# Score rows for the cluster attention from one weight-times-weight matrix per head, on one Trainium2 core

## The chip, the cores and the metric

The kernel runs on one core of one Trainium2 chip. A core has five engines, each with a queue of its own that is worked off in order: TensorE (PE in the profile; its weight loads are PEld), VectorE (DVE), ScalarE (ACT), GpSimd (POOL) and SyncE (SP), which issues the transfers. Engines meet only through semaphores. The metric is the device time of one execution in microseconds; lower is better.

## The reference, cut to what matters

32 images of 96 channels and 56x56 pixels are normalised over the channels, go through an attention with 8 heads of 48 features, and then through a feed-forward layer with quantised groups. The attention folds each image into four quarters of 28x28 pixels and works on each alone. In each quarter and head, 16 centers are the mean features of 7x7 blocks, and every pixel is compared with them:

```
f = einsum('bchw,dc->bdhw', x, Wf) + bf          # 384 features = 8 heads x 48
centers = _adaptive_avg_pool(f, 4, 4)            # 16 per head and quarter
cen_n = cen / maximum(norm(cen), EPS)
tok_n = tok / maximum(norm(tok), EPS)
sim = sigmoid(sim_beta + sim_alpha * einsum('bmc,bnc->bmn', cen_n, tok_n))
idx = argmax(sim, axis=1); sim = sim * one_hot(idx)
```

The masked `sim` then gathers the values of the pixels per center and spreads them back; `x + attention` goes on as tokens into the feed-forward layer (W1, gelu, W2, each with an absolute maximum over a group of six images).

The score of a pixel x against a center with pooled input p is x' Wf_h' Wf_h p (bias as a 97th row). The kernel never forms it from features: it makes a score row `Q` of 97 numbers for each of 8x16 centers, scales it by alpha over the center's norm, and multiplies it with the pixels.

## The kernel before, in words

A step works on one quarter. There are 128 quarters: five groups of 24 (six images, as the feed-forward layer's groups want it), and 8 more. Within a group `pipeline` runs slots; in each slot every engine runs a list of steps in the order that `attention` returns for it. A step has a phase (X first, then M, A, R) and a lag, so that one slot works on up to five quarters at once: X prepares a quarter (normalise, pool, centers, score rows), M computes features and scores, A masks, aggregates and spreads, R is the feed-forward layer's first half (tokens, their normalisation, the hidden tiles and their maxima). After the 24 slots of a group, `second_pass` runs the feed-forward layer's second half. In the groups after the first, a slot also finishes a quarter of the group before (`finish` on DVE, `clipped` on POOL). The order in an engine's queue is written out by hand; `done(engine, name, q)` makes that engine's queue wait until quarter q has passed the named step, and everything queued behind waits with it.

The steps that the change touches, in the order of the data, with the lines of the profile:

- `pooled` (DVE, L672): sums of the 16 blocks, `cenx`, 97x16.
- `centers` (PE, L925): features of the centers, 4 products with `wfT`.
- `centers` (DVE, L681): copies them to `cbd`, masked by head.
- `center_squares` (POOL, L394): `csq`, their squares.
- `center_products` (PE, L933 and L936): column sums of `csq` (the norms), and `cbd` times `wf` (the score rows), both into PSUM bank 0.
- `center_floor` (DVE, L688) and `center_norms` (POOL, L436): maximum with a floor, power -1/2.
- `q_scaled` (DVE, L693), `q_back` (PE, L958, a transposition), `q_placed` (DVE, L699): `Q`, used by `scores` of the next slot.

Around them on DVE stand `cosine` (L717, scores from PSUM times pixel norms, into `cosb`), then `residual` (L755, twice, which adds the attention's output to the image, with a hidden maximum L774 between), then `maxima` (L722, `top`). On PE, `features(0, 1)` (L969) is the next quarter's first feature tile. It writes the PSUM bank that `cosine` reads, so it begins with

```
if t0 == 0:
    done(pe, "cos_done", q - 1)
```

where q - 1 is the quarter that `cosine` handles in the same slot. `to_tokens("t")` (L906) needs `t_done` of both quarters of an image's half: in every other slot it needs the residual of this very slot.

Of the kernel before, what the change touches and what calls it, by code (L numbers as in the profile page):

```python
# [12 lines left out]
HM = HEADS * CENTERS  # L13
# [22 lines left out]
POOL_SETS = 7  # L36
DVE_SUMS, DVE_SIGNS, DVE_ALL = 4, 20, 24
# [23 lines left out]
def build(nc, x, Wf, bf, Wv, bv, Wp, bp, alpha, beta, W1, b1, W2, b2, consts, out):  # L61
# [3 lines left out]
    with ctx:  # L65
# [15 lines left out]
        cenx = sb("cenx", [C + 1, 4, CENTERS])  # L81
        cbd = sb("cbd", [C, 2, 4, 2, CENTERS])
        csq = sb("csq", [C, 2, HM])
        cn2 = sb("cn2", [HM, 2])
        cinv = sb("cinv", [HM, 2])
# [32 lines left out]
        wf = sb("wf", [C, 4, C + 1])  # L118
# [34 lines left out]
        def early(rows, *shape):  # L153
# [12 lines left out]
        NAMES = """x_side x_T x_stats x_sum x_dif x_half x_d2 x_v x_var x_rstd x_shift x_norm0 x_norm xn_ps0 xn_ps xn_copied0 xn_copied cen_x cen_f cen_bd  # L166
            cen_sq q_ps cen_n2 cen_inv q_scaled q_T q_done s_ps n2_done n2_floor n_newton0 n_square0 n_part0 n_factor0 n_newton1
# [91 lines left out]
        def _(sp):  # L259
            per_row = [(cst[:, :], consts), (w1[:, :, :], W1[0:G1 * GROUPS, :].rearrange("(g r) c -> r g c", g=GROUPS)),  # L260
                       (w2[:, :, :], W2[0:G2 * GROUPS, :].rearrange("(g r) f -> r g f", g=GROUPS)),
                       (wf[:, :, 0:C], Wf.rearrange("(k r) c -> r k c", k=4)),
                       (wv[:, :, 0:C], Wv.rearrange("(k r) c -> r k c", k=4)),
                       (wf[:, :, C:C + 1], bf.rearrange("(k r a) -> r k a", k=4, a=1)),
# [85 lines left out]
        def _(pool):  # L350
# [6 lines left out]
            nc.gpsimd.memset(uT[:, :, :, :], 0.0).then_inc(pool_set, 1)  # L357
            pool.wait_ge(pool_set, POOL_SETS)

# [28 lines left out]

            def center_squares(k, q, place, use):
                b = k % 2  # L390
                done(pool, "cen_bd", q)
                done(pool, "q_ps", q - 2)
                v = cbd[:, b, :, :, :].rearrange("c k h m -> c (k h m)")
                nc.gpsimd.tensor_tensor(csq[:, b, :], v, v, ALU.mult).then_inc(S["cen_sq"], 1)  # L394
# [36 lines left out]

            def center_norms(k, q, place, use):
                b = k % 2
                done(pool, "cen_n2", q)
                done(pool, "q_done", q - 2)
                nc.gpsimd.tensor_tensor(cinv[:, b:b + 1], cn2[:, b:b + 1], halfpow[0:HM, 0:1], ALU.pow).then_inc(S["cen_inv"], 1)  # L436
# [19 lines left out]
            def attention(g, part):  # L456
                return [(X, 1, moments("x", EPS_C)), (M, 1, norm_guess), (M, 1, newton), (M, 1, cubic),
                         (X, 1, center_squares), (R, 0, clipped(g, part), FINAL), (X, 1, center_norms),
                        (A, 0, marks), (R, 0, moments("t", EPS_T), FFN)]
# [18 lines left out]
        def _(act):  # L478
# [80 lines left out]
            def attention(part):  # L559
                return [(R, 1, normalise("t", 6, 1), FFN), (A, 1, copy_sim(0)), (R, 1, n_high(0, part), FFN),  # L560
                        (A, 1, copy_sim(1)), (R, 1, n_high(1, part), FFN), (X, 1, normalise("x", 0, 0)),
                        (X, 1, normalise("x", 0, 1)), (X, 1, copy_x(0)), (X, 1, copy_x(1)),
# [40 lines left out]
        def _(dve):  # L603
# [38 lines left out]
            for i in range(2):  # L642
                step(v.tensor_copy(V[:, 2 * i:2 * i + 2, :, 0:C],
                                   bank(4 + i, C + 1, 4 * C).rearrange("c (k h o) -> c k h o", k=2, h=2)))
            step(v.tensor_copy(w1T[0:C, 0:G1 * GROUPS], bank(6, C, G1 * GROUPS)))
# [21 lines left out]
            def pooled(k, q, place, use):  # L667

                done(dve, "xn_copied", q)
                done(dve, "u_done", q - 4)  # L670
                blocks = xn[:, k % 2, :].rearrange("c (a r b w) -> c a b r w", a=4, r=PW, b=4)
                v.tensor_reduce(cenx[:, k % 4, :].rearrange("c (a b) -> c a b", a=4), blocks, AX.XY, ALU.add)\  # L672
                    .then_inc(S["cen_x"], 1)

            def centers(k, q, place, use):

                done(dve, "cen_f", q)
                done(dve, "q_ps", q - 2)
                f = bank(0, C, 4 * CENTERS).rearrange("r (k m) -> r k m", k=4)
                mask = const("head_of_row", C)  # L680
                v.tensor_tensor(cbd[:, k % 2, :, :, :], f.unsqueeze(2).broadcast_to([C, 4, 2, CENTERS]),  # L681
                                mask.unsqueeze(1).unsqueeze(3).broadcast_to([C, 4, 2, CENTERS]), ALU.mult)\
                    .then_inc(S["cen_bd"], 1)

            def center_floor(k, q, place, use):
                done(dve, "q_ps", q)
                done(dve, "cen_inv", q - 2)
                v.tensor_scalar(cn2[:, k % 2:k % 2 + 1], bank(0, HM, 1, 64), NORM_FLOOR * AREA * AREA, None, ALU.max)\  # L688
                    .then_inc(S["cen_n2"], 1)

            def q_scaled(k, q, place, use):
                done(dve, "cen_inv", q)
                v.tensor_scalar(qT[:, :], bank(0, HM, C + 1, 128), cinv[:, k % 2:k % 2 + 1], alphac[:, :],  # L693
                                ALU.mult, ALU.mult).then_inc(S["q_scaled"], 1)

            def q_placed(k, q, place, use):
                done(dve, "q_T", q)
                done(dve, "s_ps", q - 2)
                v.tensor_copy(Q[:, k % 2, :], bank(0, C + 1, HM, 256)).then_inc(S["q_done"], 1)  # L699
# [31 lines left out]
            def summed(k, q, place, use):  # L731
                done(dve, "u_ps", q)
                done(dve, "a_ps", q - 1)
                sums = cenx[:, k % 4, :].unsqueeze(1).broadcast_to([C + 1, HEADS, CENTERS])
# [84 lines left out]
            def attention(g, part):  # L819
# [3 lines left out]
                         (X, 1, pooled), (R, 1, h_largest(4, 5), FFN), (M, 1, cosine), (X, 1, centers), (A, 1, residual(0)),  # L823
                         (R, 1, h_largest(5, 6), FFN), (A, 1, residual(1)), (X, 1, center_floor),
# [38 lines left out]
        def _(pe):  # L863
# [5 lines left out]
            mm(bank(1, G2, GROUPS), ones[0:G2, 0:G2], wsum2[:, :], start=True, stop=True)  # L869
            for k in range(4):  # L870
                tr(bank(2, C + 1, C, k * C), wf[:, k, :], ident[0:C, 0:C])
# [3 lines left out]
            for k in range(4):  # L875
                mm(bank(4 + k // 2, C + 1, 2 * C, k % 2 * 2 * C), wv[:, k, :],
                   wph[:, k, :, :].rearrange("r h o -> r (h o)"), start=True, stop=True)
            for g in range(GROUPS):
# [42 lines left out]
            def centers(k, q, place, use):  # L921
                done(pe, "cen_x", q)
                done(pe, "xn_copied", q)
                for c in range(4):
                    ins = mm(bank(0, C, CENTERS, c * CENTERS), wfT[:, c * C:(c + 1) * C], cenx[:, k % 4, :],  # L925
                             start=True, stop=True)
                ins.then_inc(S["cen_f"], 1)

            def center_products(k, q, place, use):

                done(pe, "cen_bd", q)
                done(pe, "cen_sq", q)
                mm(bank(0, HM, 1, 64), csq[:, k % 2, :], ones[0:C, 0:1], start=True, stop=True)  # L933
                n = 2 * CENTERS
                for c in range(4):
                    ins = mm(ps[c * n:(c + 1) * n, 0, 128:128 + C + 1],  # L936
                             cbd[:, k % 2, c, :, :].rearrange("r h m -> r (h m)"), wf[:, c, :], start=True, stop=True)
                ins.then_inc(S["q_ps"], 1)
# [17 lines left out]
            def q_back(k, q, place, use):  # L956
                done(pe, "q_scaled", q)
                tr(bank(0, C + 1, HM, 256), qT[:, :], ident).then_inc(S["q_T"], 1)  # L958
# [102 lines left out]
            def attention(g):  # L1061
# [5 lines left out]
                        (X, 1, centers), (A, 1, spread(1)), (M, 0, features(0, 1)), (X, 1, center_products), (X, 1, end_of_group(g), FFN),  # L1067
# [70 lines left out]
```

## Time and profile before

| | |
|---|---|
| median of 3 runs | 3020.39 us (3018.07 to 3020.47) |
| span of the profiled execution, first to last instruction | 3014.8 us |
| PE busy (matmuls / weight loads) | 95% / 64% of the span |
| DVE busy | 89% |
| ACT busy | 72% |
| POOL busy | 67% |
| mean granted TensorE clock | 0.988 of full speed |

The profiled execution has no other time than its span on the page; the median of the runs is 5.6 us longer. A row of a timeline is one or several like instructions: start, duration, engine, line, operation, tiles and shapes, and in brackets how long the engine had been idle before and what ended that. Consecutive instructions of one engine overlap a little in the records, so that the time that an instruction takes in its queue is better read from its start to the next one's start.

### The profile page before, as it was taken

Reading aid. Unit: us, or ns where it says so; the run is one execution under the profiler, and the core shown is the slowest. Engines: PE = TensorE matmul, PEld = TensorE weight load, DVE = VectorE, ACT = ScalarE, POOL = GpSimd, SP = SyncE. Lnnn points to the kernel's source line nnn. Section 1 sums busy time; section 2 is a strip of 40 time slices with the busy share of each in tenths; the row PEclk is TensorE's granted clock in tenths of the full one; section 3 lists DMA queues with packets and bytes.
Section 4 is the critical chain, followed back from the end, with each engine's and each line's share of the span. In section 5 each row is a group of like instructions: output and inputs, shape, how many; then the busy total and the mean of one; then the engine's idle time right before and its main releaser. Section 6 shows DMA issues by size and latency. Waiting matters only on the chain.

```text
span 3014.8 us, 62753 instructions
## 1 busy us (share of the span) xinstructions
PE 2860.9 (95%) x20998; PEld 1934.8 (64%) x20998; DVE 2683.4 (89%) x5540; ACT 2177.4 (72%) x4510; POOL 2014.7 (67%) x4275
## 2 busy tenths in 40 slices
PE   3999999999999999999999999999999999999987
PEld 2666666556666665666666566666665666666554
DVE  3788888999999989999999999999999999998975
ACT  1677777897767779777777886777789777777952
POOL 1566666677777768777777347777767777776354
PEclk9999999999999999999999999999999999999997
DMA  1011111002222210122222012222200222221034
GB/s 45 17 40 34 33 33 33 9 17 65 66 65 65 65 49 1 49 65 65 66 73 65 10 33 70 74 68 65 57 25 17 65 65 65 66 65 49 1 94 132
DMA packets 30932, 154.29 MB, mean 51 GB/s; under 512 B 6483, under 2 KB 6804, under 8 KB 30612
## 3 DMA queue, kind: packets, MB, share of 16 engines
q1 hardware_dynamic: 30612, 150.28, 17.8%
q8 instruction: 169, 2.77, 0.4%
q14 instruction: 151, 1.24, 0.1%
HBM read 75.60 MB, written 74.66 MB: 50 GB/s over the span
## 4 chain that ended last, share of the span: by engine, by line
POOL 58%; issue 21%; PE 13%; DVE 4%; ACT 3%; POOLq 1%; SPq 0%; DMA 0%; DVEq 0%; ACTq 0%
POOL eq L442 7%; POOL mo_x L384 6%; POOL mo_t L384 6%; PE ps L1102 4%; PE ps L1046 4%; POOL turns L468 4%; POOL tok L452 3%; POOL mo_x L379 3%; ACT turns L579 2%; POOL cinv L436 2%; POOL n2c L399 2%; DVE turns L844 2%; POOL csq L394 2%; PE ps L969 1%; POOL nxy L411 1%
## 5 line engine op out<-in xcount | busy, mean ns | idle before, releaser
L969 PE MATMUL ps<-wfT,xn 97*112 97x384 f32 x1792 | 735.9, 518 | 0.3 <-ACT sq L523 0.2
L1046 PE MATMUL ps<-tok,w1T 98*128 98x392 f16 x2880 | 599.7, 330 | 13.5 <-ACT turns L582 8.7
L523 ACT ACTIVATE sq<-ps 112x384 f32<-112x384 f32 x896 | 431.0, 489 | 207.8 <-PE ps L969 204.8
L468 POOL CAST turns<-turns 128x392 f16<-128x392 f32 x240 | 324.9, 1367 | 206.1 <-ACT turns L579 201.9
L1046 PEld LDWEIGHTS ps<-tok,w1T 98*128 98x128 f16 x2880 | 269.5, 97 | 226.1 <-issue 61.1
L707 DVE TENSOR_REDUCE n<-sq 112x32 f32<-112x1536 f32 (+1 forms) x256 | 396.0, 1547 | 20.9 <-ACT sq L523 6.8
L774 DVE TENSOR_REDUCE hmax<-ps 128x1 f32<-128x392 f32 x720 | 382.1, 558 | 33.7 <-PE ps L1046 28.1
L969 PEld LDWEIGHTS ps<-wfT,xn 97*112 97x112 f32 x1792 | 271.7, 180 | 213.9 <-DVE cosb L717 65.5
L529 ACT ACTIVATE sig<-cosb,betac 112x896 f32<-112x896 f32 x128 | 133.3, 1041 | 312.2 <-DVE cosb L717 312.2
L492 ACT ACTIVATE xnT<-ps,mo_x 112x96 f32<-112x96 f32 x896 | 304.4, 454 | 62.2 <-POOL mo_x L386 62.2
L579 ACT ACTIVATE turns<-ps,scale 128x1176 f32<-128x1176 f32 x240 | 323.0, 1346 | 36.1 <-DVE scale L797 34.5
L844 DVE SCALAR_TENSOR_TENSOR turns<-turns 128x1176 f16<-128x1176 f32 x240 | 330.2, 1376 | 0.0
L1102 PE MATMUL ps<-turns,w2T 128*96 128x392 f16 x1440 | 287.6, 336 | 22.9 <-DVE turns L844 22.8
L492 ACT ACTIVATE nT<-ps,mo_t 112x96 f32<-112x96 f32 x840 | 283.5, 438 | 28.5 <-POOL mo_t L386 28.4
L442 POOL TENSOR_TENSOR eq<-sig,top 112x896 bf16<-112x896 f32 x128 | 219.2, 1713 | 49.8 <-DVE top L722 49.8
L977 PE MATMUL ps<-Q,xn 97*112 97x128 f32 x1792 | 228.2, 279 | 24.0 <-ACT sq L523 24.0
L1102 PEld LDWEIGHTS ps<-turns,w2T 128*96 128x96 f16 x1440 | 160.0, 123 | 134.3 <-DVE turns L844 90.4
L394 POOL TENSOR_TENSOR csq<-cbd 96x128 f32<-96x128 f32 x128 | 50.7, 396 | 268.4 <-DVE cbd L681 268.4
L1009 PE MATMUL ps<-sim,xnT 112*97 112x128 f32 x1792 | 227.4, 279 | 2.4 <-ACT turns L545 2.3
L977 PEld LDWEIGHTS ps<-Q,xn 97*112 97x112 f32 x1792 | 202.5, 177 | 42.4 <-ACT sq L523 42.4
L1029 PE MATMUL ps<-turns,aggp 128*96 128x448 f32 (+1 forms) x512 | 217.6, 507 | 1.3 <-DVE aggp L746 1.3
L1009 PEld LDWEIGHTS ps<-sim,xnT 112*97 112x97 f32 x1792 | 200.1, 164 | 16.6 <-ACT turns L545 4.7
(143 smaller groups left out, 6125.8 us busy)
## 6 DMA issues: line engine op xcount, KB each, us to landing
xbuf<-in_x SPq DMA_DIRECT2D x64, 588.0 KB, 4.6
out<-xbuf SPq DMA_DIRECT2D x64, 588.0 KB, 6.0
turns<-out SPq DMA_DIRECT2D x60, 588.0 KB, 6.3
out<-turns SPq DMA_DIRECT2D x60, 588.0 KB, 4.4
tok<-in_L_ffn_W SPq DMA_DIRECT2D x2, 142.5 KB
cst<-in_constants SPq DMA_DIRECT2D x1, 195.0 KB
wf<-in_L_conv_Wf SPq DMA_DIRECT2D x1, 144.0 KB
tok<-in_L_conv_Wv SPq DMA_DIRECT2D x1, 144.0 KB
```

The lines of the kernel that those rows point to most:

```text
L442: nc.gpsimd.tensor_tensor(heads(eq[:, :]), heads(sig[:, k % 2, :]), over_centers(top[:, :]), ALU.subtract)\
L468: nc.gpsimd.tensor_copy(ghi[:, k % 3, HT:2 * HT], gel[:, k % 3, HT:2 * HT]).then_inc(b_mid, 1)
L492: ins = nc.scalar.activation(dst, bank(b0 + part, TN, C, (t - t0) * C), ACT.Identity, bias=m[:, 9, t:t + 1], scale=m[:, 8, t:t + 1])
L523: nc.scalar.activation(sq[:, t, :], bank(2 + t % 2, TN, D), ACT.Square).then_inc(f_sq, 1)
L579: nc.scalar.activation(gel[:, k % 3, :].rearrange("p (c n) -> p c n", c=FC), ps[:, h:h + 3, 0:HT], ACT.Gelu, scale=scale[:, 0:1]).then_inc ...
L707: ins = v.reduce_sum(n2[:, t0 * HEADS:t1 * HEADS], sq[:, t0:t1, :].rearrange("p t (h d) -> p (t h) d", d=HD), AX.X)
L844: v.scalar_tensor_tensor(glo[:, k % 2, :], gel[:, k % 3, :], QCLIP, ghi[:, k % 3, :], ALU.min, ALU.subtract).then_inc(b_lo, 1)
L969: mm(bank(2 + t % 2, TN, D), xn[:, k % 2, t * TN:(t + 1) * TN], wfT[:, :], start=True, stop=True)\
L977: ins = mm(tile_bank(2, TN, HM, t), xn[:, k % 2, t * TN:(t + 1) * TN], Q[:, k % 2, :], start=True, stop=True)
L1009: ins = mm(bank(4, C + 1, HM), xnT[:, k % 4, t, :], sim[:, k % 2, t * HM:(t + 1) * HM], start=t == 0, stop=t == T - 1)
L1046: ins = mm(dst, w1T[:, c * 128:(c + 1) * 128], tok[:, bass.ds(place, 1), part, s * HT:(s + 1) * HT].rearrange("p a n -> p (a n)"), start=p ...
L1102: ins = mm(bank(6 + k % 2, C, HT), w2T[:, c, :], part[:, s, c * HT:(c + 1) * HT], start=n == 0, stop=n == 2 * FC - 1)
```

## The change

For each head, a matrix G = Wf_h' Wf_h (97x97, bias included) is made once at the start: 8 products on PE and two copies on DVE, with `wf` laid out by heads. `center_products` then makes the unscaled score rows straight from `cenx` and G (8 products of 97x32 weights, as `project` does it elsewhere), with a padded `cenx` in place of the masked `cbd`, at the place in PE's queue where `centers` stood. The steps `centers` (PE and DVE), `center_squares` and `center_floor` go. New are: `spread_centers` (POOL, `cenx` repeated for 8 heads into `cenr`), `copy_products` (ACT, score rows to SBUF, `qU`), `centers_turned` (PE, a transposition of `cenr`, at the place where `center_products` stood, behind `features(0, 1)`), and on DVE `center_norms`, which multiplies the turned centers with the score rows and sums over the 97 columns: that sum is the squared norm. It stands where `centers` stood on DVE, between `cosine` and `residual(0)`. POOL now does the floor itself, ahead of the power.

```diff
+            def center_norms(k, q, place, use):
+
+                done(dve, "cen_T", q)
+                done(dve, "q_side", q)
+                done(dve, "cen_floor", q - 2)
+                b = k % 2
+                v.tensor_tensor_reduce(cprod[:, :], bank(0, HM, C + 1, 256), qU[:, :], 1.0, 0.0, ALU.mult, ALU.add,
+                                       accum_out=cn2[:, b:b + 1]).then_inc(S["cen_n2"], 1)
...
-                         (X, 1, pooled), (R, 1, h_largest(4, 5), FFN), (M, 1, cosine), (X, 1, centers), (A, 1, residual(0)),
-                         (R, 1, h_largest(5, 6), FFN), (A, 1, residual(1)), (X, 1, center_floor),
+                         (X, 1, pooled), (R, 1, h_largest(4, 5), FFN), (M, 1, cosine), (X, 1, center_norms), (A, 1, residual(0)),
+                         (R, 1, h_largest(5, 6), FFN), (A, 1, residual(1)),
...
+            def spread_centers(k, q, place, use):
+                done(pool, "cen_x", q)
+                done(pool, "cen_T", q - 1)
+                nc.gpsimd.tensor_copy(heads(cenr[:, :]), cenx[:, k % 4, 1, :].unsqueeze(1).broadcast_to([C + 1, HEADS, CENTERS]))\
+                    .then_inc(S["cen_r"], 1)
...
+            def copy_products(k, q, place, use):
+                done(act, "q_ps", q)
+                done(act, "q_scaled", q - 1)
+                nc.scalar.copy(qU[:, :], bank(0, HM, C + 1, 128)).then_inc(S["q_side"], 1)
...
+            for h in range(HEADS):
+                mm(bank(h // 4, C + 1, C + 1, h % 4 * (C + 1)), wf[:, h, :], wf[:, h, :], start=True, stop=True)
...
-            def centers(k, q, place, use):
+            def centers_turned(k, q, place, use):
+                done(pe, "cen_r", q)
+                done(pe, "q_side", q)
+                tr(bank(0, HM, C + 1, 256), cenr[:, :], ident[0:C + 1, 0:C + 1]).then_inc(S["cen_T"], 1)
+
+            def center_products(k, q, place, use):
                 done(pe, "cen_x", q)
                 done(pe, "xn_copied", q)
...
+                n, turned = 2 * CENTERS, cenx[:, k % 4, :, :].rearrange("c s m -> c (s m)")
+                for h in range(2):
+                    for c in range(4):
+                        ins = mm(ps[c * n:(c + 1) * n, 0, 128:128 + C + 1], turned[:, (1 - h) * CENTERS:(1 - h) * CENTERS + n],
+                                 G[:, 2 * c + h, :], start=h == 0, stop=h == 1)
                 ins.then_inc(S["q_ps"], 1)
...
-                        (X, 1, centers), (A, 1, spread(1)), (M, 0, features(0, 1)), (X, 1, center_products), (X, 1, end_of_group(g), FFN),
+                        (X, 1, center_products), (A, 1, spread(1)), (M, 0, features(0, 1)), (X, 1, centers_turned), (X, 1, end_of_group(g), FFN),
```

On PE, in a slot of a middle group, from the last hidden tile (L1046, after: L1053) to the image's tokens (`xbuf`), the queue was

```order
L1046 MATMUL ps<-tok,w1T 128x392 x2
L925 MATMUL ps<-cenx,wfT 96x16 x4
L1029 MATMUL ps<-turns,aggp 96x336
L969 MATMUL ps<-wfT,xn 112x384
L933 MATMUL ps<-cst,csq 128x1
L936 MATMUL ps<-wf,cbd 32x97 x4
L969 MATMUL ps<-wfT,xn 112x384
L906 MATMUL ps<-cst,xbuf 112x96 x7
```

and it is, at the same place,

```order
L1053 MATMUL ps<-tok,w1T 128x392 x2
L943 MATMUL ps<-G,cenx 32x97 x8
L1036 MATMUL ps<-turns,aggp 96x336
L976 MATMUL ps<-wfT,xn 112x384
L935 MATMUL ps<-cst,cenr 128x97
L976 MATMUL ps<-wfT,xn 112x384
L917 MATMUL ps<-cst,xbuf 112x96 x7
```

The score rows moved ahead of the first feature tile (`wfT,xn`); what stands behind it now is the transposition of `cenr`.

On DVE, in the same slot, from `cosine` (`cosb`) to the scaled score rows (`qT`), the queue was

```order
L717 TENSOR_TENSOR cosb<-ps,ninv 112x896
L681 TENSOR_TENSOR cbd<-ps,cst 96x128
L755 SCALAR_TENSOR_TENSOR xbuf<-ps,bpc,xbuf 96x16x28
L774 TENSOR_REDUCE hmax<-ps 128x1
L755 SCALAR_TENSOR_TENSOR xbuf<-ps,bpc,xbuf 96x12x28
L688 TENSOR_SCALAR cn<-ps 128x1
L722 TENSOR_REDUCE top<-sig 112x56
L693 TENSOR_SCALAR qT<-ps,cinv,alphac 128x97
```

and it is

```order
L725 TENSOR_TENSOR cosb<-ps,ninv 112x896
L695 ISA cprod,cn<-ps,qU 128x97
L695 ISA cn 128x1
L763 SCALAR_TENSOR_TENSOR xbuf<-ps,bpc,xbuf 96x16x28
L782 TENSOR_REDUCE hmax<-ps 128x1
L763 SCALAR_TENSOR_TENSOR xbuf<-ps,bpc,xbuf 96x12x28
L730 TENSOR_REDUCE top<-sig 112x56
L701 TENSOR_SCALAR qT<-qU,cinv,alphac 128x97
```

Two single instructions went (`cbd`, `cn`), and two came: the product with its sum, and a second instruction that writes the sum out. They stand in front of both residuals, and they wait for the PE row `cst,cenr`.

## Rows read from the trace of the kernel before

**Rows 1.** The profile's page, parts 1 and 2: busy us and share; granted clock by slices.
```profile
span 3014.8 us, 62753 instructions
PE 2860.9 (95%) x20998; PEld 1934.8 (64%) x20998; DVE 2683.4 (89%) x5540; ACT 2177.4 (72%) x4510; POOL 2014.7 (67%) x4275
...
PEclk9999999999999999999999999999999999999997
```

**Rows 2.** Timeline of DVE, one slot of a middle group: start, us, instruction [idle before].
```profile
1919.23 1.08 DVE L717 TENSOR_TENSOR cosb<-ps,ninv 112x896 f32<-112x896 f32 x1
1920.22 0.28 DVE L681 TENSOR_TENSOR cbd<-ps,cst 96x128 f32<-96x128 f32 x1
1920.42 0.67 DVE L755 SCALAR_TENSOR_TENSOR xbuf<-ps,bpc,xbuf 96x448 f32<-96x448 f32 x1
...
1921.96 0.14 DVE L688 TENSOR_SCALAR cn<-ps 128x1 f32<-128x1 f32 x1
1922.03 1.07 DVE L722 TENSOR_REDUCE top<-sig 112x56 f32<-112x896 f32 x1
...
1927.00 1.25 DVE L663 BATCH_NORM_STATS2 st_x<-ps 112x6 f32<-112x96 f32 x7 [0.19 <-PE ps L906]
...
1931.62 1.19 DVE L766 TENSOR_TENSOR tok<-ps,tok 98x448 f16<-98x448 f32 x2 [0.17 <-ACT tok L556]
1933.02 0.29 DVE L735 SCALAR_TENSOR_TENSOR uT<-cenx,ps 97x128 f32<-97x128 f32 x1 [0.21 <-PE ps L1009]
...
1935.05 1.04 DVE L774 TENSOR_REDUCE hmax<-ps 128x1 f32<-128x392 f32 x2 [0.23 <-PE ps L1046]
...
1937.50 1.08 DVE L717 TENSOR_TENSOR cosb<-ps,ninv 112x896 f32<-112x896 f32 x1
```

**Rows 3.** Timeline of PE, the same slot.
```profile
1915.31 0.54 PE L1019 MATMUL ps<-V,uT 97*32 97x97 f32 x16
...
1918.89 0.85 PE L925 MATMUL ps<-cenx,wfT 97*96 97x16 f32 x8
1919.59 0.79 PE L1029 MATMUL ps<-turns,aggp 128*96 128x336 f32 x2
1920.37 0.90 PE L969 MATMUL ps<-wfT,xn 97*112 97x384 f32 x2
...
1921.71 0.90 PE L969 MATMUL ps<-wfT,xn 97*112 97x384 f32 x2
1922.45 0.74 PE L906 MATMUL ps<-cst,xbuf 96*112 96x96 f32 x7
1923.03 1.47 PE L969 MATMUL ps<-wfT,xn 97*112 97x384 f32 x4
1924.33 0.27 PE L958 MATMUL ps<-cst,qT 128*97 128x128 f32 x1
...
1931.21 1.77 PE L1009 MATMUL ps<-sim,xnT 112*97 112x128 f32 x14
```

**Rows 4.** Timeline of POOL, the same slot.
```profile
1923.18 1.71 POOL L442 TENSOR_TENSOR eq<-sig,top 112x896 bf16<-112x896 f32 x1 [0.42 <-DVE top L722]
...
1928.13 0.21 POOL L386 TENSOR_TENSOR mo_t<-mo_t 112x7 f32<-112x7 f32 x1
```

**Rows 5.** Timeline of ACT, the same slot.
```profile
1920.34 1.04 ACT L529 ACTIVATE sig<-cosb,betac 112x896 f32<-112x896 f32 x1 [2.51 <-DVE cosb L717]
...
1928.37 2.36 ACT L492 ACTIVATE nT<-ps,mo_t 112x96 f32<-112x96 f32 x7 [0.22 <-POOL mo_t L386]
```

**Rows 6.** The chain that ended last, whole span: the same place of the first group's slots.
```profile
146.30 2.58 issue
...
548.26 2.58 issue
```

**Rows 7.** The same chain, from 20 to 60 us: the preparation of the weights.
```profile
33.43 2.88 PE ps L876 x8
...
40.47 0.57 DVE V L643
```

More of the change, by code:

```diff
@@ L35 @@
 LOADS = 14
-POOL_SETS = 7
-DVE_SUMS, DVE_SIGNS, DVE_ALL = 4, 20, 24
+POOL_SETS = 8
+DVE_SUMS, DVE_SIGNS, DVE_ALL = 4, 20, 26
 CONSTS = {}
@@ L80, in build @@
         xn = sb("xn", [C + 1, 2, QN])
-        cenx = sb("cenx", [C + 1, 4, CENTERS])
-        cbd = sb("cbd", [C, 2, 4, 2, CENTERS])
-        csq = sb("csq", [C, 2, HM])
+        cenx = sb("cenx", [C + 1, 4, 3, CENTERS])
+        cenr = sb("cenr", [C + 1, HM])
+        qU = sb("qU", [HM, C + 1])
+        cprod = sb("cprod", [HM, C + 1])
         cn2 = sb("cn2", [HM, 2])
+        cfl = sb("cfl", [HM, 2])
         cinv = sb("cinv", [HM, 2])
@@ L387, in moments @@
                 return step
[L389 to L394, printed above, removed]
             def norm_guess(k, q, place, use):
@@ L457, in attention @@
                 return [(X, 1, moments("x", EPS_C)), (M, 1, norm_guess), (M, 1, newton), (M, 1, cubic),
-                         (X, 1, center_squares), (R, 0, clipped(g, part), FINAL), (X, 1, center_norms),
+                         (X, 1, spread_centers), (R, 0, clipped(g, part), FINAL), (X, 1, center_norms),
                         (A, 0, marks), (R, 0, moments("t", EPS_T), FFN)]
@@ L644, in _ @@
                                    bank(4 + i, C + 1, 4 * C).rearrange("c (k h o) -> c k h o", k=2, h=2)))
+            for i in range(2):
+                step(v.tensor_copy(G[:, 4 * i:4 * i + 4, :],
+                                   bank(i, C + 1, 4 * (C + 1)).rearrange("c (h o) -> c h o", h=4)))
             step(v.tensor_copy(w1T[0:C, 0:G1 * GROUPS], bank(6, C, G1 * GROUPS)))
@@ L671, in pooled @@
                 blocks = xn[:, k % 2, :].rearrange("c (a r b w) -> c a b r w", a=4, r=PW, b=4)
-                v.tensor_reduce(cenx[:, k % 4, :].rearrange("c (a b) -> c a b", a=4), blocks, AX.XY, ALU.add)\
+                v.tensor_reduce(cenx[:, k % 4, 1, :].rearrange("c (a b) -> c a b", a=4), blocks, AX.XY, ALU.add)\
                     .then_inc(S["cen_x"], 1)
-            def centers(k, q, place, use):
[L677 to L689, printed above, removed]
+            def center_norms(k, q, place, use):
[5 more added lines that the diff above has]
+                                       accum_out=cn2[:, b:b + 1]).then_inc(S["cen_n2"], 1)
             def q_scaled(k, q, place, use):
                 done(dve, "cen_inv", q)
-                v.tensor_scalar(qT[:, :], bank(0, HM, C + 1, 128), cinv[:, k % 2:k % 2 + 1], alphac[:, :],
+                done(dve, "q_T", q - 1)
+                v.tensor_scalar(qT[:, :], qU[:, :], cinv[:, k % 2:k % 2 + 1], alphac[:, :],
                                 ALU.mult, ALU.mult).then_inc(S["q_scaled"], 1)
@@ L877, in _ @@
                    wph[:, k, :, :].rearrange("r h o -> r (h o)"), start=True, stop=True)
+            for h in range(HEADS):
+                mm(bank(h // 4, C + 1, C + 1, h % 4 * (C + 1)), wf[:, h, :], wf[:, h, :], start=True, stop=True)
             for g in range(GROUPS):
```

40 lines of the change are left out of this document (16 added, 24 removed).

## The prediction, made before the changed kernel was run

> **What bounds the kernel now.** I began with the page's busy shares [rows 1]: TensorE is busy 95% of the span, VectorE 89%. So full an engine invites the thought that work taken off it is time won. But a busy TensorE is not one at its peak, so I went on to the timelines of one slot, engine by engine, and asked at each place who waits for whom.
>
> A slot takes 18.27 us: from one `cosine` to the next it is 1937.50 - 1919.23 [rows 2]. In the first group it is the same, (548.26 - 146.30) / 22 = 18.27 [rows 6], though VectorE and GpSimd have less to do there (nothing to finish, nothing to clip). So neither of these two is bound by the sum of its work. What both kinds of slot share is a ring of waits, which the rows show link by link. I set `cosine`'s start to 0 (1919.23):
>
> - `cosine` runs to 1.08; behind it on VectorE stand `cbd` at 0.99, the first residual at 1.19, the second, the floor `cn` at 2.73, and `top` at 2.80 to 3.87 [rows 2].
> - GpSimd's `eq` starts at 3.95, having idled 0.42 for `top` [rows 4]. The moments of the tokens follow without a pause and end at 9.11.
> - ScalarE starts `nT` at 9.14, having idled 0.22 for these moments [rows 5]. Behind `nT` in its queue stands the copy of the turned similarities, and for that copy TensorE's aggregation (L1009) waits; it starts at 11.98 [rows 3].
> - VectorE's `uT` waits 0.21 for the aggregation, and its hidden maxima 0.23 for the hidden tiles behind it on TensorE [rows 2]. From there VectorE runs through to the next `cosine` at 18.27.
>
> Every handover has an engine idle just before it, so the ring has no slack. It passes through VectorE's stretch from `cosine` to `top`, 2.80 us. Whatever makes this stretch longer makes the slot longer by as much, and TensorE's feature tiles, the turning of the marks and the scores are not on the ring at all: they only have to be done in time.
>
> **The change, part by part.**
>
> *TensorE.* The features of the centers took 0.70 (1918.89 to 1919.59) [rows 3]; the 16 passes that replace them have the shape of `project` (L1019), 0.54. The stretch from one feature tile to the next, with the norms and the score rows between, is 1.34 (1920.37 to 1921.71). A feature tile alone is 0.65, half of the 1.30 that two take (1923.03 to 1924.33), and a transposition as L958 lasts 0.27, so it becomes at most 0.92. TensorE sheds 0.58 a slot at least. But L1029 ends and `features(0, 1)` then waits for `cosine` in either kernel (it starts 0.06 behind it, at 1.14), so what is saved in front of it turns into a longer wait, and what is saved behind it lies off the ring. I count it as nothing.
>
> *VectorE, the work.* `cbd` goes: 0.20 from its start to the residual's. `cn` goes: 0.07 to `top` [rows 2]. The product with its sum is an instruction that this trace does not have. The order shows it as two, one of 128x97 and one of a single column. The nearest rows are the two that go: 0.20 and 0.07, 0.27 together, if both overlap with what follows as those do; 0.28 + 0.14 = 0.42 if they are worked off one after the other. I take 0.35, since the second reads what the first leaves. The Trainium skill says the same of the pair ("VectorE: DVE Perf Modes", the section on two Vector instructions with no wait between them: an operation that also writes its accumulator out is two instructions); it gives no time for the second, and no row here has one.
>
> *VectorE, the wait.* This is the term that decides. `center_norms` stands right behind `cosine` on VectorE. It waits for `centers_turned`, which stands on TensorE behind `features(0, 1)`, which waits for `cosine`. So VectorE sends its result to TensorE and can go on only when TensorE has done a whole feature tile and a transposition: 1.08 (end of `cosine`) + 0.06 + 0.65 + 0.27 = 2.06, and 0.04 more until VectorE starts (`uT` starts 0.04 behind the end of L1009 in the trace, 1933.02 against 1931.21 + 1.77) [rows 2, 3]. The product starts at 2.10, where `cbd` started at 0.99. Queued behind it are both residuals, a hidden maximum and `top`.
>
> The residual then starts at 2.10 + 0.35 = 2.45 in place of 1.19. From it to `cn` it is 1.54 (1920.42 to 1921.96), so `top` starts at 3.99 in place of 2.80. **The ring grows by 1.19**, from 18.27 to 19.46. With 0.27 and 0.42 for the product it is 1.11 and 1.26.
>
> *The covers.* The turned centers also need two other engines. ScalarE copies the score rows: these are done at 1918.89 + 0.54, that is 0.20, while ScalarE idles for `cosine` until 1.11 [rows 5]. Even at the price of the `sig` behind it (1.04 for nine times the columns) the copy ends at 1.28, before the 1.79 at which TensorE wants it. GpSimd repeats the centers as soon as the pooled sums are there, by -0.34 (L925 waited for the same); at the price of `eq` (1.71, a far larger tile) that is 1.4, still in time. Floor and power come after the product, 2.45; at 1.71 for both they end by 4.2, and `qT` is not wanted before `top` ends at about 5. In every other slot the tokens on TensorE wait for the second residual, which now ends near 3.99; they started at 3.22, so TensorE is 0.8 late there, less than the 1.19 that the ring gives it.
>
> *Outside the slots.* G costs 8 products of 97 columns at the start; the four of 192 there take 2.88 [rows 7], so about 2.9, and two copies of 0.57 and a few transpositions: +4.5, once. The 12 quarters' slots that have no feed-forward half (4 at the start, 8 at the end) are not on the ring. There TensorE's saving may count and the same stall may too: between -1.2 and +1.2 for each, ±14 in all; I take -2 for them, a little toward the saving, as there is little else on the engines there.
>
> *The sum.* 120 slots x 1.19 = 143, + 4.5 - 2 = 145 on the span of 3014.8: 3160. The median of the runs lies 5.6 above the span; I leave that as it is: 3020.4 + 145 = **3165**.
>
> **The rivals.**
>
> *A: TensorE is the bound.* It is 95% busy, and sheds 0.58 a slot: -0.58 x 120 = -70, +4.5, so 2955. For it speaks the share; against it the ring, and that `features(0, 1)` waits for `cosine` anyway. It decides if the aggregation on TensorE was waiting for its own queue and not for ScalarE, and if VectorE can take in 1.1 of idle time. VectorE's idle time in a slot is 0.19 + 0.17 + 0.21 + 0.23 = 0.80 [rows 2], less than that, so I give it 4%.
>
> *B: only VectorE's own time counts.* If the link through GpSimd and ScalarE had slack after all, the longer stretch would first eat the 0.80 that VectorE idles later. Then 1.19 - 0.80 = 0.39 is left in the 96 slots of the later groups and nothing in the first, where VectorE has a microsecond less to do: +37, + 2.5, so 3060. Against it: `uT` itself waits for the aggregation, the far end of that link. 10%.
>
> *C: occupancy.* The wait is hidden in some way that I do not see, and VectorE pays for its work alone: 0.35 - 0.27 = 0.08 more in 128 slots, +10, and +2.5: 3033. The Trainium skill ("Perfetto Trace Analysis", Identifying the Most-Contended Engine) goes by occupancy for VectorE and calls matmul busy time a poor measure, which would make VectorE the engine to watch and leave it at that. The trace disagrees in so far as the first group's VectorE has less to do in a slot of equal length. 3%.
>
> *D: the clock.* TensorE's granted clock is full in nearly all slices [rows 1]. Longer idle times in each slot might bring it down to the lower of its two levels, 1.2 GHz. The feature tile and the transposition in the stall would then take 0.92 longer: 120 x 0.92 = +110, so 3275. It decides if the idle time before the tokens, at most 4.0 - 2.0 = 2 in every other slot, is enough for it; nothing in the slots of this trace is so long. 5%.
>
> **How the numbers follow.** The ring with the stall has the remaining 78%: 3165, from 120 x 1.11 + 2.5 - 14 = +122 to 120 x 1.26 + 2.5 + 14 = +168, that is 3142 to 3188. For 8 in 10 I widen it a little on both sides, toward part of B below and part of D above: 3125 to 3205. This kernel's measurement can tell about 0.2%, 6 us, from no change. Faster by more is A, 4%; no change would need C with a smaller price, 2%; slower is the rest, 94%.
>
> **What would show it.** In the profile after, VectorE idles about 1.0 in front of the product in every slot, put down to TensorE's row on `cenr`, some 120 us in all. `top` starts near 4.0 behind `cosine`, and slots follow at 19.4 to 19.5 in the first group as in the others. GpSimd still idles for `top`, ScalarE for the moments. TensorE's busy share falls, the second passes keep their length, the clock stays. I am wrong if slots stay near 18.3 with that idle time in them (there was slack in the ring), if it is missing, or if the product costs much more than 0.4.

## The result and the profile after

The changed kernel takes 3157.25 us (median of 4 runs, 3151.06 to 3159.38), the kernel before 3020.43 on the same chip: ratio 1.0451, interval 1.0436 to 1.0466. The span went from 3014.8 [rows 1] to 3149.2, by 134.4. The page of the kernel after, parts 1 and 2, shows every engine with a smaller share of a longer span:

```profile
span 3149.2 us, 62927 instructions
PE 2835.7 (90%) x20890; PEld 1845.6 (59%) x20890; DVE 2667.6 (85%) x5542; ACT 2210.8 (70%) x4638; POOL 2032.1 (65%) x4404
...
PEclk9999999999999999999999999999999999999988
```

TensorE and VectorE are busy 25 and 16 us less than in [rows 1], and the kernel is 134 us slower. So the time is in waits. The timeline of DVE, one slot of a middle group, as in [rows 2]:

```profile
1982.58 1.08 DVE L725 TENSOR_TENSOR cosb<-ps,ninv 112x896 f32<-112x896 f32 x1
1984.73 0.26 DVE L695 CUSTOM_DVE_ANT_0 cprod<-ps,qU 128x97 f32<-128x97 f32 x1 [1.07 <-PE ps L935]
1984.92 0.08 DVE L695 DVE_READ_ACCUMULATOR2_ANT cn<- 128x1 f32 x1
1984.92 0.68 DVE L763 SCALAR_TENSOR_TENSOR xbuf<-ps,bpc,xbuf 96x448 f32<-96x448 f32 x1
...
1986.46 1.07 DVE L730 TENSOR_REDUCE top<-sig 112x56 f32<-112x896 f32 x1
1987.45 0.32 DVE L701 TENSOR_SCALAR qT<-qU,cinv,alphac 128x97 f32<-128x97 f32 x1
...
1997.48 0.29 DVE L743 SCALAR_TENSOR_TENSOR uT<-cenx,ps 97x128 f32<-97x128 f32 x1 [0.21 <-PE ps L1016]
...
2001.96 1.08 DVE L725 TENSOR_TENSOR cosb<-ps,ninv 112x896 f32<-112x896 f32 x1
```

With `cosine` at 0, the product starts at 2.15 and the residual at 2.34; `top` starts at 3.88, where it was at 2.80 [rows 2], and the next `cosine` at 19.38, where it was at 18.27. What the product waits for is the row L935 of TensorE, in the same stretch (beside [rows 3]):

```profile
1982.27 0.54 PE L943 MATMUL ps<-G,cenx 97*32 97x97 f32 x16
1982.74 0.81 PE L1036 MATMUL ps<-turns,aggp 128*96 128x336 f32 x2
1983.71 0.90 PE L976 MATMUL ps<-wfT,xn 97*112 97x384 f32 x2 [0.16 <-DVE cosb L725]
1984.45 0.25 PE L935 MATMUL ps<-cst,cenr 97*128 97x97 f32 x1
1984.53 0.82 PE L976 MATMUL ps<-wfT,xn 97*112 97x384 f32 x2
1986.21 0.76 PE L917 MATMUL ps<-cst,xbuf 96*112 96x96 f32 x7 [0.86 <-DVE hmax L782]
```

The transposition L935 stands behind a feature tile L976 that waited for `cosine`; and the tokens L917 now wait 0.86 for VectorE, an idle time that [rows 3] did not have. Downstream the links of the ring are the same and late by the same 1.1. First GpSimd, then ScalarE (beside [rows 4, 5]):

```profile
1985.08 0.24 POOL L438 TENSOR_SCALAR cfl<-cn 128x1 f32<-128x1 f32 x1 [1.56 <-DVE cn L695]
1985.40 0.57 POOL L442 TENSOR_TENSOR cinv<-cfl,halfpow 128x1 f32<-128x1 f32 x1
1987.61 1.73 POOL L448 TENSOR_TENSOR eq<-sig,top 112x896 bf16<-112x896 f32 x1 [1.64 <-DVE top L730]
```

```profile
1982.88 0.24 ACT L535 COPY qU<-ps 128x97 f32<-128x97 f32 x1 [1.70 <-PE ps L943]
...
1992.84 2.36 ACT L498 ACTIVATE nT<-ps,mo_t 112x96 f32<-112x96 f32 x7 [0.90 <-POOL mo_t L390]
```

`eq` starts at 5.03 (3.95 before), `nT` at 10.26 (9.14 before). GpSimd and ScalarE both idled longer for their link, so neither had become the cause. The view of waits of the whole program after (us in total, times, longest):

```profile
...
POOL eq L448 <- DVE top L730: 191.3, 118, 1.6
DVE cprod L695 <- PE ps L935: 134.7, 123, 2.7
...
ACT nT L498 <- POOL mo_t L390: 79.0, 112, 1.0
```

That the wait of `cprod` adds up to 134.7, almost the loss itself, is partly chance. In a slot it is 1.07; with the product's 0.19, less the 0.20 of `cbd` and the 0.07 of `cn`, and with the 0.09 by which `cbd` began before `cosine` was over, `top` is late by 1.08. The rest of the 1.11 is added on GpSimd behind `eq`: the moments end 1.12 later than before, and `nT` starts 1.12 later with them.

Where the 134.4 lie, from the starts of all 128 `cosine` rows in both traces (what follows the last of them takes 22.9 before and 23.0 after):

| | before | after | difference |
|---|---|---|---|
| start of the span to the first `cosine` | 73.57 | 76.53 | +3.0 |
| first three slots | 55.7 | 55.0 | -0.7 |
| 115 regular slots (median 18.27, 19.38) | 2102.0 | 2234.3 | +132.3 |
| five stretches between groups | 668.3 | 664.5 | -3.8 |
| last four slots | 92.3 | 95.9 | +3.6 |

Of the 115 regular slots five took 20.5 to 20.6 after, and five took 18.4 before. In the five after, TensorE ran slower from the tokens on, for some 4 us. Timeline of PE, the slot that follows the one shown, which is one of them:

```profile
2005.98 1.27 PE L917 MATMUL ps<-cst,xbuf 96*112 96x96 f32 x7 [1.24 <-DVE xbuf L763]
2007.04 2.71 PE L976 MATMUL ps<-wfT,xn 97*112 97x384 f32 x4
```

The two feature tiles (a tile is two rows) take 2.71 where such a group takes 1.47 [rows 3]; the idle time ahead is 1.24. From 2006 to 2008 us the granted clock is 0.53 of full speed, near the lower of its two levels (1.2 of 2.4 GHz), and before 2006 and behind 2010 us it is 1.00. TensorE idles 1.24 in front of the tokens in every second slot (55 of them), and behind five of these its clock fell; behind the 0.86 of the others it never did. These five slots are 6 us of the loss.

### The profile page after: what moved, and what is told of

Same layout as the page of the kernel before. It is cut to its first block, busy times and chain, and to the rows that moved or that the text cites. A ratio compares the mean times of both kernels' runs of the same rounds, so it can differ in the third digit from the quotient of the medians.

```text
span 3149.2 us, 62927 instructions
## 1 busy us (share of the span) xinstructions
PE 2835.7 (90%) x20890; PEld 1845.6 (59%) x20890; DVE 2667.6 (85%) x5542; ACT 2210.8 (70%) x4638; POOL 2032.1 (65%) x4404
## 4 chain that ended last, share of the span: by engine, by line
PE 48%; POOL 18%; DVE 11%; issue 11%; ACT 10%; SPq 0%; POOLq 0%; DMA 0%; DVEq 0%; ACTq 0%
PE ps L1053 11%; PE ps L976 8%; PE ps L1016 7%; PE ps L1109 4%; ACT nT L498 4%; PE ps L984 3%; PE ps L928 3%; POOL eq L448 3%; POOL turns L474 3%; POOL mo_t L388 3%; PE ps L1046 3%; DVE xbuf L763 2%; POOL tok L458 2%; DVE cosb L725 2%; ACT turns L590 2%
## 5 line engine op out<-in xcount | busy, mean ns | idle before, releaser
L976 PE MATMUL ps<-wfT,xn 97*112 97x384 f32 x1792 | 723.5, 517 | 19.7 <-DVE cosb L725 19.4
L1053 PE MATMUL ps<-tok,w1T 98*128 98x392 f16 x2880 | 599.8, 330 | 13.0 <-ACT turns L593 8.2
L976 PEld LDWEIGHTS ps<-wfT,xn 97*112 97x112 f32 x1792 | 273.9, 182 | 241.4 <-DVE cosb L725 87.6
L1053 PEld LDWEIGHTS ps<-tok,w1T 98*128 98x128 f16 x2880 | 269.3, 97 | 225.7 <-issue 61.0
L1109 PE MATMUL ps<-turns,w2T 128*96 128x392 f16 x1440 | 287.0, 335 | 22.9 <-DVE turns L852 22.9
L774 DVE TENSOR_TENSOR tok<-ps,tok 98x448 f16<-98x448 f32 x240 | 135.7, 566 | 103.1 <-ACT tok L567 96.5
L917 PE MATMUL ps<-cst,xbuf 96*112 96x96 f32 x840 | 95.2, 255 | 121.4 <-DVE xbuf L763 69.0
```

The source lines that it names most:

```text
L976: mm(bank(2 + t % 2, TN, D), xn[:, k % 2, t * TN:(t + 1) * TN], wfT[:, :], start=True, stop=True)\
L1053: ins = mm(dst, w1T[:, c * 128:(c + 1) * 128], tok[:, bass.ds(place, 1), part, s * HT:(s + 1) * HT].rearrange("p a n -> p (a n)"), start=p ...
L1109: ins = mm(bank(6 + k % 2, C, HT), w2T[:, c, :], part[:, s, c * HT:(c + 1) * HT], start=n == 0, stop=n == 2 * FC - 1)
```

## The experiments

The theory, as predicted (**ring**): the slot is a ring of waits without slack, and the product's wait, which stands in the ring between `cosine` and `top`, lengthens it by its full size. Rivals: TensorE or VectorE is full (**occupancy**), or the new work itself costs the time, wherever it stands. Each ratio is to the kernel before on the same chip. The median of the kernel before was 3023.67 there, but 3025.34 for the two last kernels (after_psum and turned_early_mid_psum), 3020.09 for norms_late_psum, norms_mid and turned_early_mid, and 3010.03 for after_half and the two extra kernels.

**turned_early: TensorE's queue mended.** The transposition moves ahead of the feature tile; VectorE's order and all the work stay.

```diff
-(X, 1, center_products), (A, 1, spread(1)), (M, 0, features(0, 1)), (X, 1, centers_turned), ...
+(X, 1, center_products), (A, 1, spread(1)), (X, 1, centers_turned), (M, 0, features(0, 1)), ...
```

> The changed kernel with one step moved on TensorE: the transposition of the centers stands ahead of features(0, 1) instead of behind it, so that it no longer waits for cosine. Ring theory: the idle time in front of the product is gone, from cosine to top it is 0.99 + 0.19 + 1.54 = 2.72 in place of 3.88, the slot goes from 19.38 to about 18.2 and the time to 3010 to 3022. Rival, the new instructions and copies themselves are what costs: still about 3155. Rival, TensorE is the bound and its saved work now counts: 0.58 a slot below the kernel before, about 2955.

Measured: 3021.25, ratio to before 0.9985 (0.9975 to 0.9996). The slot is 18.33. VectorE's timeline there has no idle time left in front of the product:

```profile
1958.33 1.08 DVE L725 TENSOR_TENSOR cosb<-ps,ninv 112x896 f32<-112x896 f32 x1
1959.43 0.26 DVE L695 CUSTOM_DVE_ANT_0 cprod<-ps,qU 128x97 f32<-128x97 f32 x1
...
1961.16 1.07 DVE L730 TENSOR_REDUCE top<-sig 112x56 f32<-112x896 f32 x1
```

`top` is back at 2.83. All the instructions of the change are still there; only one place in TensorE's queue differs, and of the 1.11 a slot 0.06 is left. It was the wait, not the work. It was not a gain either: the regular slots are not shorter than before, so what TensorE shed bought nothing in them. Where the 0.15% of the ratio lies is not shown.

**norms_late: VectorE's queue mended instead.** The product moves behind both residuals, by when L935 is done.

```diff
-... (M, 1, cosine), (X, 1, center_norms), (A, 1, residual(0)),
-(R, 1, h_largest(5, 6), FFN), (A, 1, residual(1)),
+... (M, 1, cosine), (A, 1, residual(0)),
+(R, 1, h_largest(5, 6), FFN), (A, 1, residual(1)), (X, 1, center_norms),
```

> The changed kernel with one step moved on VectorE: the product with its sum stands behind the second residual, where the floor stood before the change, and not behind cosine. Ring theory: the turned centers are there at 2.1, the product is reached at 2.5, so nothing waits; cosine to top is 2.72, the slot 18.2, the time 3010 to 3022, as with the transposition moved. Rival, the transposition's place on TensorE (it still delays the second feature tile) or the new work costs: 3060 to 3155.

Measured: 3167.79, ratio 1.047 (1.0455 to 1.0486), with slots of 19.55. A miss: `top` came at 2.72 as expected, and the slot was a little longer than in the changed kernel. DVE's timeline shows where the time went, and POOL's, in the fence behind it, what stood beside it:

```profile
1985.76 1.07 DVE L730 TENSOR_REDUCE top<-sig 112x56 f32<-112x896 f32 x1
1986.84 1.85 DVE L701 TENSOR_SCALAR qT<-qU,cinv,alphac 128x97 f32<-128x97 f32 x1
1988.61 1.24 DVE L677 BATCH_NORM_STATS2 st_t<-ps 112x6 f32<-112x96 f32 x7
```

```profile
1986.91 1.71 POOL L448 TENSOR_TENSOR eq<-sig,top 112x896 bf16<-112x896 f32 x1
1989.93 0.23 POOL L375 TENSOR_TENSOR mo_t<-st_t 112x14 f32<-112x14 f32 x1 [1.31 <-DVE st_t L677]
```

The scaling `qT` takes 1.85 instead of the 0.32 of the kernel after, and ends where `eq` ends (1988.69 and 1988.62). The statistics of the tokens stand behind it, and GpSimd, done with `eq`, idles 1.31 for them: a second wait on the same ring. In this kernel `qT` reads `qU` in SBUF, as the change has it (before, it read PSUM), and since `cinv` ends just ahead of `eq`, `qT` and `eq` start together. In the regular slots of the kernel after, `qT` starts 0.16 ahead of `eq` and escapes.

**norms_late_psum** is norms_late with one operand changed: `qT` reads the score rows where TensorE left them.

```diff
-v.tensor_scalar(qT[:, :], qU[:, :], cinv[...
+v.tensor_scalar(qT[:, :], bank(0, HM, C + 1, 128), cinv[...
```

> The changed kernel with the product behind the second residual, as in norms_late, and the scaling to qT reading the score rows from PSUM instead of the copy in SBUF. Theory, the shared port: in norms_late qT took 1.85 in place of 0.32 because it read SBUF while GpSimd's eq held the port; from PSUM it takes 0.37 again, the slot falls from 19.55 to about 18.25, the time to 3010 to 3025. Rival, qT was long because the norm came late from GpSimd: still 19.5 and about 3165.

Measured: 2998.6, ratio 0.9922 (0.9901 to 0.9943), slots 18.19, faster than the kernel before by 0.8%, and a little below what was expected. DVE's row, and POOL's:

```profile
1934.67 0.38 DVE L701 TENSOR_SCALAR qT<-ps,cinv,alphac 128x97 f32<-128x97 f32 x1
```

```profile
1934.74 1.72 POOL L448 TENSOR_TENSOR eq<-sig,top 112x896 bf16<-112x896 f32 x1
```

The same start beside `eq`, 0.07 ahead of it, and 0.38 instead of 1.85. So the operand in SBUF is the cause. The Trainium skill ("SBUF — State Buffer", section SBUF: two separate sides) has a shared port pair of VectorE and GpSimd that one instruction holds to its end while the other fully blocks. The trace agrees with the block: `qT` was held for the length of `eq`. The page gives the pair to whoever starts first; by the profile's start times VectorE's row was first and yet lost, so the recorded start does not tell who got it. No semaphore stands between `qT` and `eq`: the first section says that engines meet only through semaphores, and here one held the other up without one.

**norms_mid** puts the product between the two residuals, with all else as in the changed kernel:

```diff
-... (M, 1, cosine), (X, 1, center_norms), (A, 1, residual(0)),
-(R, 1, h_largest(5, 6), FFN), (A, 1, residual(1)),
+... (M, 1, cosine), (A, 1, residual(0)),
+(R, 1, h_largest(5, 6), FFN), (X, 1, center_norms), (A, 1, residual(1)),
```

> The changed kernel with the product one place earlier than in norms_late, between the hidden maximum and the second residual, qT from SBUF as in the change. The turned centers come at 2.10, the place is reached at 2.05; the norm is ready by 3.4, before top ends, so qT starts ahead of eq. Ring theory: cosine to top 2.77, slot about 18.25, 3010 to 3025. Rival, the place of the product does not matter as long as the transposition stands behind the feature tile: above 3060.

Measured: 3022.36, ratio 1.0001 (0.999 to 1.0012), slots 18.31, `top` at 2.82. Far enough back to find L935 done, far enough ahead for `qT` to begin 0.16 before `eq`: it lasts 0.32.

**before_stall: the wait without the change.** The kernel before, with nothing else of the change: in nearly every slot the first residual also waits until the first feature tile behind `cosine` is done.

```diff
+if half == 0 and q % GQ != 1 and q + 2 < GROUPS * GQ + BODY:
+    dve.wait_ge(f_ps, (q + 2) * T + 1)
```

> The kernel before, with nothing of the change but a wait: VectorE's first residual waits for the first feature tile of the quarter that follows, which on TensorE waits for cosine. Ring theory: the tile is done 1.08 + 0.06 + 0.90 + 0.04 = 2.08 behind cosine's start, the residual starts there in place of 1.19, +0.89 in each of some 119 slots, 3126. Rival, the slower time came from the new work: 3020. Rival, VectorE's later idle time of 0.80 a slot takes it in: 3020 to 3035.

Measured: 3125.67, ratio 1.0325 (1.0307 to 1.0343), slots 19.17. VectorE's timeline:

```profile
1949.17 1.08 DVE L717 TENSOR_TENSOR cosb<-ps,ninv 112x896 f32<-112x896 f32 x1
...
1951.24 0.68 DVE L757 SCALAR_TENSOR_TENSOR xbuf<-ps,bpc,xbuf 96x448 f32<-96x448 f32 x1 [0.80 <-PE ps L971]
...
1968.33 1.08 DVE L717 TENSOR_TENSOR cosb<-ps,ninv 112x896 f32<-112x896 f32 x1
```

The residual starts at 2.07 in place of 1.19, 0.88 later, and the slot is 0.89 longer by these rows (19.16). A wait alone, with no instruction added, costs its full length. The 0.80 that VectorE idles elsewhere in the slot absorbed none of it, as rival B needs it to.

**extra_in_ring and extra_off_ring: the same work in two places.** The kernel before with one more reduction of 112x448 on VectorE into a tile that nobody reads; once ahead of `top`, once behind `masked`, off the ring.

```diff
+v.tensor_reduce(junk[:, :], heads(sig[:, k % 2, 0:T * HM // 2]), AX.X, ALU.max)
...
+(A, 0, extra), (A, 0, maxima), (X, 1, q_scaled), ...        # extra_in_ring
...
+(X, 0, stats("x", 0)), (A, 0, masked), (A, 0, extra), ...   # extra_off_ring
```

> The kernel before with one more VectorE instruction a slot, a maximum over half of the similarities into an unused tile (about 0.52 from start to next start, half of what top takes), placed between the second residual's floor and top. Ring theory: it is on the ring, the slot grows by all of it, 18.8, about 3082. Rival, VectorE's sum of work or its idle time decides: the same time as with the instruction placed elsewhere, 3020 to 3050.

> The same additional VectorE instruction, placed behind the masking of the similarities instead, off the ring; VectorE idles 0.17 + 0.21 + 0.23 = 0.61 behind that place. Ring theory: it is taken in, the slot stays at 18.27, 3020 to 3030. Rival, VectorE's sum of work decides: as long as with the instruction ahead of top.

Measured in the ring: 3081.45, ratio 1.0239 (1.0205 to 1.0273), slots 18.82. Off it: 3024.27, ratio 1.0036 (1.0016 to 1.0056), slots 18.29 to 18.34. Against the 3010.03 of the kernel before on that chip these are 71 and 14 us. VectorE's row in the first and in the second kernel, the same instruction:

```profile
1962.08 0.60 DVE L728 TENSOR_REDUCE junk<-sig 112x28 f32<-112x448 f32 x1
1962.60 1.07 DVE L723 TENSOR_REDUCE top<-sig 112x56 f32<-112x896 f32 x1
```

```profile
1962.92 0.60 DVE L728 TENSOR_REDUCE junk<-sig 112x28 f32<-112x448 f32 x1
```

It pushes `top` back by 0.52 in the first, and the slot grows by 0.55. In the second it costs about 0.05 a slot: not quite nothing, but a tenth. By occupancy both should cost the same.

**before_half and after_half: TensorE's largest work halved.** From the program's third quarter on, both kernels compute only 192 of the 384 feature columns of a tile; the other half is left out, so the norms of the pixels, which are made from these columns, are no longer the reference's.

```diff
+n = D if q < 2 else D // 2
-mm(bank(2 + t % 2, TN, D), xn[:, k % 2, t * TN:(t + 1) * TN], wfT[:, :], ...
+mm(bank(2 + t % 2, TN, n), xn[:, k % 2, t * TN:(t + 1) * TN], wfT[:, 0:n], ...
```

> The kernel before, leaving out half of the feature columns (192 of 384) from the third quarter on: TensorE does 7 x 0.32 = 2.3 us less in a slot, everything else the same. Ring theory: the feature tiles are not on the ring, the slot stays at 18.2 to 18.27, 3005 to 3020. Rival, TensorE is the bound: up to 2.3 less in 120 slots, down to 2750.

> The changed kernel, leaving out half of the feature columns from the third quarter on. Ring theory: one of the seven feature tiles, the first, stands in the stall between cosine and the product, so the slot falls by its half, 0.32, to 19.05, and the time by about 38 to 3119; the other six tiles give nothing. Rival, TensorE is the bound: up to 2.3 less a slot, 2890. Rival, the stall is something else than that tile: 3157.

Measured without the change: 3022.08, ratio 0.9995 (0.9982 to 1.0008), slots 18.28 to 18.34. So TensorE's work bought nothing there, and rival A is out: an engine that the page shows 95% busy was not the bound.

With the change: 3179.49, ratio 1.0559 (1.0525 to 1.0593). Expected were 3119, a miss by the total; by the ratios this kernel is 1% slower than the kernel after (1.0451). The slots that nothing disturbs take 19.07, as expected, since the product now waits for half a tile. But about half of all slots take 20.1 to 20.2, and the granted clock over the span is 0.907. Windows of 10 us of after_half (columns: length, busy time of PE, PEld, DVE, ACT and POOL, granted clock, DMA share, GB/s):

```profile
1950.00:1960.00 10.00, 10.00 (x72) 9.51 (x71) 7.76 (x16) 7.20 (x19) 8.16 (x22) 0.69 0.00 1
1960.00:1970.00 10.00, 8.43 (x75) 5.31 (x73) 8.88 (x23) 5.89 (x14) 5.24 (x13) 0.99 0.01 3
1970.00:1980.00 10.00, 9.72 (x69) 8.97 (x68) 7.90 (x18) 7.12 (x19) 8.48 (x22) 0.67 0.30 88
```

In the stretch at 0.99 TensorE is busy 8.43 of 10 us, with one long idle time in front of the tokens, as its timeline has it:

```profile
1967.61 0.76 PE L917 MATMUL ps<-cst,xbuf 96*112 96x96 f32 x7 [1.18 <-DVE hmax L782]
```

In the next stretch it gets 0.67, and the slot is 1.1 longer. In front of the tokens TensorE idles 1.18 in one slot and 1.56 in the next, where the kernel after has 0.86 and 1.24. Of the slots with 1.18, 25 of 60 took 20.1 or more; of those with 1.56, 28 of 55. before_half leaves out the same columns and never idles in front of the tokens, and its granted clock over the span is 0.979 (0.988 in the kernel before). So with the same work left out, the kernel with the stall loses its clock and the one without it hardly does. That is the mechanism of rival D, in a kernel that idles more than the predicted one. The two ran on different chips, and the idle time was not varied by itself, so this cause is argued and not shown.

**The tail, and the best version.** **turned_early_mid** makes both moves (turned_early's and norms_mid's).

> Both moves: the transposition ahead of features(0, 1) and the product between the hidden maximum and the second residual. Ring theory: no wait at all, cosine to top is 2.80 - 0.20 - 0.07 + 0.19 = 2.72, the slot 18.19, 0.08 below the kernel before, 3008 to 3018; TensorE's 0.58 a slot stay without effect. Rival, TensorE was the bound in part: below 3000.

Measured: 3008.81, ratio 0.996 (0.9946 to 0.9974), slots 18.21. That is 10 us more than norms_late_psum at a slot only 0.02 longer, and the difference lies in the last four slots: 94.0 against 79.5. There the tokens are clipped on GpSimd ahead of `cinv`, so `qT` and `eq` come together again. DVE's row and POOL's in the last slots of turned_early_mid, and DVE's in norms_late_psum:

```profile
2920.21 1.72 DVE L701 TENSOR_SCALAR qT<-qU,cinv,alphac 128x97 f32<-128x97 f32 x1 [1.73 <-POOL cinv L442]
```

```profile
2920.15 1.71 POOL L448 TENSOR_TENSOR eq<-sig,top 112x896 bf16<-112x896 f32 x1
```

```profile
2918.76 0.38 DVE L701 TENSOR_SCALAR qT<-ps,cinv,alphac 128x97 f32<-128x97 f32 x1 [1.63 <-POOL cinv L442]
```

Two kernels take the operand alone: **after_psum** is the changed kernel with `qT` from PSUM, **turned_early_mid_psum** the same on top of both moves. Their edit is the one line of norms_late_psum.

> The changed kernel as it is, but the scaling of the score rows reads them where TensorE left them, in PSUM, and not ScalarE's copy in SBUF. Ring theory with the shared port: in the slots of the groups the scaling begins before eq and nobody holds it up, so slots stay at 19.38 and the product stays 1.07 late. In the last four slots of the changed kernel the scaling lasts 1.72 beside eq instead of 0.32, and the transposition behind it waits; from PSUM it should last about 0.38 there, worth 3 to 5 us for each of these slots as norms_late_psum (19.7 to 19.9 against 23 to 24) has it. Sum: 3157 - 16 = 3141 (3136 to 3148). Rival, the source of the operand matters in every slot: slots of 19.2 or less, some 3120 or below. Rival, the last slots are long for another reason: 3155 to 3160.

> Both moves, and the scaling of the score rows from PSUM. Ring theory with the shared port: slots of 18.2 as in turned_early_mid, top at 2.72, the last four slots short by the same 3 to 5 us each, so 3009 - 13 = 2996 (2990 to 3002), the same as norms_late_psum within the measurement. Rival, norms_late_psum is faster for where its product stands and not for the operand: this one then stays at 3005 to 3012.

Measured: after_psum 3138.54, ratio 1.0389 (1.0366 to 1.0411). Its regular slots stay at 19.38 and its last four take 79.7 in place of 95.9, as expected: reading the operand from SBUF beside `eq` costs the changed kernel 16 us in its last four slots, and leaves the regular slots as they are. turned_early_mid_psum took 2983.93 (2980.68 to 2992.51), ratio 0.9869 (0.9848 to 0.989), faster than the kernel before by 1.3% and the fastest here; its slots are 18.19, the last four 79.5. That is 6 us below the expected range. Its profiled execution took 2992.51, inside it. Slots do not tell it from norms_late_psum; in the profiled executions the five stretches between groups do, with 665.1 against 671.0, each of them near 130 or near 134 (the last near 137). Why one execution gets the shorter and another the longer stays open.

## Why the prediction was right, step by step

**The ring has no slack: right.** before_stall charged a bare wait in full, extra_in_ring a bare instruction, extra_off_ring a tenth of it for the same instruction (0.05 a slot), before_half nothing for half of TensorE's feature work. Rivals A, B and C are out; the first group's slots are 19.37 like the others, where B wanted no growth.

**The product's start: right.** 2.10 predicted, 2.15 measured, behind the tile and the transposition that were named (from the tile's start to the transposition's it is 0.74, where I had 0.65). turned_early shows that this wait is the loss.

**The product's price: mis-sized.** I took 0.35, between 0.27 and 0.42. From the product's start to the residual's it is 0.19, below both ends; the rows last 0.26 and 0.08, but the read of the accumulator starts together with the next instruction and costs the queue nothing. My reason for 0.35, that the second reads what the first leaves, did not hold. So the ring grew by 1.11 and not 1.19: `top` came at 3.88, not 3.99. Over the 115 regular slots that is 9 us too much, and counting 120 slots is another 6. The sum is over by only 10.6, since the five slots with the lower clock, for which it had no term, gave 6 back; that these cancel in part is luck.

**TensorE's saving counted as nothing: right.** By the starts of its rows it shed more than the 0.58 that I had put as the least: from L943 to the next row it is 0.47, where L925 took 0.70, and from one feature tile to the next, with the transposition between, 0.82 in place of 1.34, together 0.75. Yet its busy time in a slot fell only from 18.04 to 17.92 (windows from `cosine` to `cosine`): the rest of its rows spread over the longer slot, one more case of a busy TensorE that is not one at its peak. Where the wait is gone, in turned_early, the saving bought nothing in the slots: 18.33 against 18.27.

**The covers: right in the slots, one left out.** `qU`'s copy (0.24), `cenr` (0.29), `cfl` (0.24) and `cinv` (0.57) all end before they are wanted. That `qT` now reads SBUF was in the diff and in the order that I showed, and I gave it no price. In the regular slots it had none; in the last four it is 16 us by after_psum. That the sum did not suffer is luck: before, these slots lost as much elsewhere (92.3), since `cinv` stood behind the clipping and `qT` started at 6.2, against 5.1 after.

**Outside the slots: right.** +4.5 predicted, +3.0 measured up to the first `cosine`. For the rest I had -2; the gaps, the first three and the last four slots give -0.9 together.

**The clock: right for the forecast, not without it.** I gave 5% to a clock that falls in every slot, behind an idle time of up to 2 in front of the tokens in every other slot. This idle time is 1.24, and 0.86 in the slots between, where I had none; the clock fell in five of 115 slots, for 6 us. after_half shows that with 1.56 and 1.18, and half of the feature columns, it falls in about half of them.

Sum: +132.3 + 3.0 - 0.7 - 3.8 + 3.6 = 134.4 measured on the span, 145 predicted.

## What to carry to other kernels

Before pricing an instruction, ask what it waits for and what is queued behind it: here two instructions of 0.3 us together cost 4.5%, because they stood at the head of an in-order queue and waited for a result behind an unrelated tile on another engine. Where a slot is a ring of waits, busy shares don't tell what a change is worth; follow the ring, and test it with the same instruction inside and outside of it. When an operand moves from PSUM to SBUF, look at what GpSimd does beside it.

## What the hardware showed that I had not expected

A scaling of 128x97 on VectorE that lasts 0.32 took 1.72 to 1.85 when it met GpSimd's `eq` with its operand in SBUF, and 0.38 beside the same `eq` with the operand in PSUM. The read of the accumulator cost VectorE's queue nothing measurable. And the changed kernel with half of the feature columns, where TensorE idles 1.18 and 1.56 in front of the tokens in place of 0.86 and 1.24, had a granted clock of 0.907 over the span in place of 0.984, and was slower with less to do. In the changed kernel itself the clock fell behind the idle time of 1.24 in 5 of 55 slots, and behind 0.86 in none of 60.
